# Attention scores in a macaron transformer block: the row minimum of tiles 2 and 3 taken with the sum over the relative scores, tile 0's scores in one product, a new order of the work

## The reference

```
x = x + 0.5 * ffn(layernorm(x))
x = x + attention(layernorm(x))
x = x + 0.5 * ffn(layernorm(x))

ffn(x) = sum over 8 experts of (silu(x @ Wg[e]) * (x @ Wu[e])) @ Wd[e]        # 128 -> 512 -> 128

attention, 16 heads of 8 features:
q, k = rotary(x @ w_q.T) / sqrt(8), rotary(x @ w_k.T);  v = x @ w_v.T
rel[i, j] = rel_emb[clip(j - i, -32, 32) + 32]
scores = q k^T + q . rel[i, j], causal;  p = softmax(scores)
ctx = p v + sum_j p[i, j] rel[i, j];  out = ctx @ w_o.T
```

## Time and profile before

| | us |
|---|---|
| median of 3 runs | 1436.86 (1435.93 to 1439.6) |
| the profiled execution, its own time | 1438.3 |
| its span | 1436.5 |
| TensorE busy | 1375.4 (96%) |
| VectorE busy | 1278.3 (89%) |
| ScalarE busy | 1101.9 (77%) |
| GpSimd busy | 1087.4 (76%) |

### The profile page before, as it was taken

One profiled execution on the slowest core, in us unless ns is written; L12 is line 12 of the kernel. 1 busy time (PEld: TensorE's weight loads), 2 busy tenths in 40 slices (PEclk: granted clock), 3 DMA queues, 4 the chain that ended last, 5 costly groups with the idle time before them and its releaser, 6 DMA issues.

```text
span 1436.5 us, 29572 instructions
## 1 busy us (share of the span) xinstructions
PE 1375.4 (96%) x8632; PEld 1076.9 (75%) x8632; DVE 1278.3 (89%) x2541; ACT 1101.9 (77%) x2642; POOL 1087.4 (76%) x956
## 2 busy tenths in 40 slices
PE   8999999999999999999999999999999999999898
PEld 7787676777777777777777778777777777778686
DVE  6887898999999999999999989899999999899565
ACT  6656778878778887788888878778887778788454
POOL 7967787787778877887778768787777877677555
PEclk9999999999999999999999999999999999999999
DMA  6404999999999999999999999899999999897200
GB/s 185 142 15 125 154 192 187 178 204 170 180 188 175 165 178 176 187 160 189 164 152 209 170 167 179 148 191 177 171 172 161 192 162 173 161 173 142 44 1 8
DMA packets 718386, 225.08 MB, mean 157 GB/s; under 512 B 652305, under 2 KB 697745, under 8 KB 718225
## 3 DMA queue, kind: packets, MB, share of 16 engines
q1 hardware_dynamic: 556224, 172.45, 72.9%
q10 hardware_dynamic: 162000, 50.75, 19.4%
HBM read 60.95 MB, written 69.86 MB: 91 GB/s over the span
## 4 chain that ended last, share of the span: by engine, by line
PE 47%; DVE 19%; ACT 9%; issue 7%; DMA 6%; ACTq 4%; SPq 4%; POOL 3%; POOLq 0%; DVEq 0%
PE work L708 9%; PE work L710 9%; PE work L709 9%; PE acc L786 5%; PE acc L787 4%; DVE hid L1071 4%; PE acc L791 4%; DMA probs_t<-probs 4%; DVE hid L1065 3%; DVE negmax L1167 3%; ACTq L1000 3%; PE work L839 3%; DVE work L1162 3%; ACT work L960 2%; DVE probs L1176 2%
## 5 line engine op out<-in xcount | busy, mean ns | idle before, releaser
L1218 POOL TENSOR_TENSOR hid_lo<-hid,hid_hi 128x512 fp32r<-128x512 f32 x512 | 663.5, 1302 | 215.6 <-ACT hid_hi L915 115.1
L909 ACT ACTIVATE hid<-work 128x512 f32<-128x512 f32 x512 | 310.1, 606 | 123.9 <-PE work L710 84.9
L1065 DVE SCALAR_TENSOR_TENSOR hid<-hid,work 128x512 f32<-128x512 f32 x512 | 345.7, 680 | 53.9 <-ACT hid L909 53.4
L1071 DVE TENSOR_TENSOR hid<-hid,work 128x512 f32<-128x512 f32 x512 | 346.6, 680 | 33.6 <-PE work L710 31.2
L915 ACT CAST hid_hi<-hid 128x512 fp32r<-128x512 f32 x512 | 320.1, 630 | 49.7 <-DVE hid L1071 30.8
L786 PE MATMUL acc<-hid_hi,wd 128*128 128x512 f32 x512 | 216.5, 423 | 12.4 <-ACT hid_hi L915 9.9
L1167 DVE TENSOR_REDUCE negmax<-work 128x1 f32<-128x384 f32 (+3 forms) x352 | 219.2, 634 | 1.2
L1233 POOL TENSOR_TENSOR probs<-exps,probs 128x512 f16<-128x512 f32 (+1 forms) x160 | 172.0, 1075 | 62.8 <-ACT probs L972 59.8
L708 PE MATMUL work<-xt,wg 128*128 128x512 f32 x512 | 207.0, 404 | 5.4 <-DVE xt L1040 1.5
L708 PE MATMUL work<-xt,wu 128*128 128x512 f32 x512 | 206.1, 402 | 2.8 <-DVE hid L1071 1.9
L791 PE MATMUL acc<-hid_lo,wd 128*128 128x512 f32 x512 | 204.1, 401 | 1.0 <-POOL hid_lo L1218 0.7
(11 more groups left out here) (97 smaller groups left out, 2184.5 us busy)
## 6 DMA issues: line engine op xcount, KB each, us to landing
prob_window_scratch<-probs SPq DMA_DIRECT2D x384, 80.0 KB, 3.5
rel_win<-rel_window_scratch ACTq DMA_DIRECT2D x250, 96.0 KB, 4.3
q_scratch<-rope SPq DMA_DIRECT2D x16, 512.0 KB, 4.2
qq<-q_scratch ACTq DMA_DIRECT2D x32, 256.0 KB
rel_window_scratch<-g_s SPq DMA_DIRECT2D x32, 256.0 KB, 5.1
k_scratch<-rope SPq DMA_DIRECT2D x16, 512.0 KB, 4.2
kk<-k_scratch ACTq DMA_DIRECT2D x32, 256.0 KB
prob_window_scratch<-probs SPq DMA_DIRECT2D x32, 256.0 KB, 3.2
```

The costliest lines, as they stand in the source:

```text
L909: act.activation(hid[:, arg % HB, :], work[bank_of["gate", arg]][:, :], ACT.Tanh, scale=0.5).then_inc(s_tanh, 1)
L1065: dve.scalar_tensor_tensor(out=hid[:, arg % HB, :], in0=hid[:, arg % HB, :], scalar=1.0, in1=work[bank_of["gate", arg]][:, :], op0=ALU.add ...
L1071: dve.tensor_tensor(hid[:, arg % HB, :], hid[:, arg % HB, :], work[bank_of["up", arg]][:, :], ALU.mult).then_inc(s_hid, 1)
L1218: pool.tensor_tensor(hid_lo[:, arg % 2, :], hid[:, arg % HB, :], hid_hi[:, arg % 2, :].bitcast(F32), ALU.subtract).then_inc(s_hlo, 1)
```

## The change

For tiles 2 and 3, `largest` now reduces only the keys that no window covers, 224 of 384 and 352 of 512 columns, into a new small tile `far`, and waits only for the scores. `near` then runs behind it as one `tensor_tensor_reduce`: it adds the window to the last 160 columns and takes the minimum of the results and of `far` at once, into `negmax`. The exponential of these tiles waits for `near`, and `shifted` follows `near`. Tiles 0 and 1 keep their order and forms.

Tile 0's scores are one product with the operands exchanged: the queries of the tile are stationary and the padded keys of all four heads (512 columns) move. So `q_pad` of tile 0 pads the keys and waits for their load. That of tile 1 waits for the queries' load.

The planner gets new durations for some steps, the dependencies of the above, no `after_short`, and a new table `LATER`.

```diff
-    LATER = {"acc": -30.5, "attention_sum": -109.4, "band_turn": -104.1, "band_values": 13.2, "down": -3.2,
...
+    LATER = {"acc": -126.3, "attention_sum": -93.6, "band_turn": 15.6, "band_values": 3.2, "down": -3.3,
...
-        step("ACT", 0.7, time, "ln_scaled", what, ("ln_shift", what))
+        step("ACT", 1.54, time, "ln_scaled", what, ("ln_shift", what))
...
-        step("PE", 0.9, end + 24, "project_v", t, ("ln_lo", ("ln2", t)))
+        step("PE", 1.3, end + 24, "project_v", t, ("ln_lo", ("ln2", t)))
...
-            step("ACT", 0.3, first - 28, "load_q", gg, ("qk_store", (t, 0)), ("qrel", back(gg, 2)),
+            step("ACT", 0.5, first - 28, "load_q", gg, ("qk_store", (t, 0)), ("qrel", back(gg, 2)),
...
-            step("ACT", 0.3, first - 14, "load_k", gg, ("qk_store", (t, 1)),
+            step("ACT", 0.5, first - 14, "load_k", gg, ("qk_store", (t, 1)),
...
-                step("ACT", 0.55, max(begin - 13, first - 13), "load_window", quad, ("qrel_store", gg),
+                step("ACT", 0.85, max(begin - 13, first - 13), "load_window", quad, ("qrel_store", gg),
...
-                step("POOL", 1.0, begin - 6, "q_pad", quad, ("load_q", gg),
+                step("POOL", 1.0, begin - 6, "q_pad", quad, ("load_q" if i else "load_k", gg),
...
-                step("ACT", 0.3, due[last_of(quad)] + 5, "load_band", quad, ("store_band", last_of(quad)),
+                step("ACT", 0.35, due[last_of(quad)] + 5, "load_band", quad, ("store_band", last_of(quad)),
...
-                 ("load_k", quad // NT), done_with(back(k, 2)))
-            step("DVE", 0.07 + HEADS[i] * (P if i == 0 else W) / (960 if i < 2 else 580), due[k] + 0.5, "near", k, ("scores", k),
-                 ("load_window", quad))
-            step("DVE", wide(columns), due[k] + 0.7, "largest", k, ("near", k))
-            step("ACT", HEADS[i] * 0.235 + columns / 1200, due[k] + 1, "exp", k, ("largest", k),
+                 ("load_q", quad // NT), ("load_k", quad // NT), done_with(back(k, 2)))
+            step("DVE", 0.07 + HEADS[i] * (P if i == 0 else W) / (960 if i < 2 else 500), due[k] + 0.5, "near", k, ("scores", k),
+                 ("load_window", quad), ("largest", k if i > 1 else None))
+            step("DVE", wide(columns if i < 2 else i * P - R), due[k] + 0.7, "largest", k, ("near" if i < 2 else "scores", k))
+            step("ACT", HEADS[i] * 0.235 + columns / 1200, due[k] + 1, "exp", k, ("largest" if i < 2 else "near", k),
...
-        if name in ("gate", "up", "down", "down_lo", "project") and (start > clock["PE"] or after_short):
+        if name in ("gate", "up", "down", "down_lo", "project") and start > clock["PE"]:
             takes += 0.1
-        if engine == "PE":
-            after_short = name == "scores" and TASKS[arg % NK][1] < 2
...
+        far = sb("negmax_far", [P, 4])
...
                     if places[0] == 0:
                         pe.wait_ge(s_qp, quad + 1)
-                    for n, a in enumerate(places):
-                        done = pe.matmul(bank[:, n * keys:(n + 1) * keys], q_pad[:, quad % 2, a, :],
-                                         kk[:, gg % 2, 0:keys], start=True, stop=True)
+                    if i == 0:
+                        pe.wait_ge(s_qld[gg % 2], 16 * (gg // 2 + 1))
+                        done = pe.matmul(bank[:, :], qq[:, gg % 2, 0:P], q_pad[:, quad % 2, :, :].rearrange(
+                            "p a k -> p (a k)"), start=True, stop=True)
+                    else:
+                        for n, a in enumerate(places):
+                            done = pe.matmul(bank[:, n * keys:(n + 1) * keys], q_pad[:, quad % 2, a, :],
+                                             kk[:, gg % 2, 0:keys], start=True, stop=True)
...
-                    act.wait_ge(s_max, arg + 1)
+                    act.wait_ge(s_max if i < 2 else s_near, arg + 1)
...
+                    else:
+                        dve.wait_ge(s_max, arg + 1)
+                        dve.tensor_tensor_reduce(out=near[:, :, 0], in0=near[:, :, 0], in1=window_of[:, :, 0],
+                                                 op0=ALU.add, op1=ALU.min, scale=1.0, scalar=far[:, arg % 4:arg % 4 + 1],
+                                                 accum_out=negmax[:, place:place + 1]).then_inc(s_near, 1)
...
+                    else:
+                        dve.wait_ge(s_sc, arg + 1)
+                        dve.tensor_reduce(far[:, arg % 4:arg % 4 + 1], heads[:, 0, 0:i * P - R], AX.X, ALU.min).then_inc(s_max, 1)
...
                     if i == 0:
+                        pool.wait_ge(s_kld[gg % 2], 16 * (gg // 2 + 1))
+                    if i == 1:
                         pool.wait_ge(s_qld[gg % 2], 16 * (gg // 2 + 1))
...
+                    source = (qq if i else kk)[:, gg % 2, i * P:(i + 1) * P]
```

## The result

The changed kernel took 1458.4 us (median of 5 runs, 1442.45 to 1462.67) against 1435.93 us before on the same chip: a ratio of 1.0139, with a 95% interval of 1.0108 to 1.0169. On a second occasion, beside other kernels, it was 1451.87 against 1435.74, 1.0122 (1.0081 to 1.0163). It is slower. I had forecast 1423 with a range that ended at 1446. The profiled execution took 1442.45 us (span 1440.6), so it is the kernel's fastest run, and its profile shows less of the loss than the median has.

The account below looks back on a forecast made before the run. VectorE, 93% busy in attention with TensorE beside it, was taken as near the limit. Half of VectorE's 21 us and TensorE's 7 us, 14 us, with due times at 0, gave 1423 us; range 1404 to 1446.

Parts of the forecast that it names:

- The parts: Shorter reductions remove 41.6 us from VectorE, the new sum adds 20.5; tile 0's single product removes 7 us from TensorE.
- The pair's net: VectorE's reduction and sum in tiles 2 and 3 together save 21 us, between 42 saved and 10 lost.
- How much of it reaches the end: Share of the engines' savings that shortens the run: half, giving 14 us off.
- the chain's 23%: Share of the two VectorE instructions' busy time on the chain that ended last, taken as the low end.
- my half: Half of VectorE's and TensorE's savings reaches the end, with VectorE 93% busy and TensorE beside it.
- The due times at nothing: The new table and durations rearrange all five lists; taken as 0, between 9 us gained and 18 us lost.
- the loose end from the stages: If all attention stages were as loose on VectorE as the first, attention would grow by 1.5%, 18 us.
- My sentence on the DMA queues: The new order adds or removes no traffic: the DMA queues carry the same 225 MB.
- The slower rival: GpSimd's tile-0 padding waits for a late keys' load, delaying its queue: 24 us lost, 1447 us; chance 0.14, including looser order.
- My signs of being wrong: Sum stepping over 0.5 us, q_pad waiting over 14 us for keys, or TensorE's ScalarE and GpSimd stalls absorbing VectorE's saving.
- The accumulator eats it: VectorE's new sum costs 0.2 us more, a net loss of 10 us there: 1438 us; chance 0.12.
- all of it counts: VectorE sets the pace and the order is as dense as the best stage: 34 us off, 1403 us; chance 0.08.

Follow-up runs that it names:

- experiment 5: Kernel before, lists untouched, with the two new VectorE instructions in place and the window's load issued behind the exponential: 1428.16 against 1435.74 us, 0.9954.
- experiment 6: Kernel before with tiles 2 and 3 reducing 160 columns fewer into an unread tile, their exponentials taking a constant: 1428.22 against 1435.74 us, 0.9943.
- experiment 10: Kernel before, its lists moved little, with both new VectorE instructions, window load behind the exponential, and tile 0 in one product: 1426.57 against 1434.2 us, 0.9935.
- experiment 3: Changed kernel's lists with the old sum, reduction, four tile-0 products and padded queries: 1449.27 against 1434.71 us, 1.0099.
- The mended queue: Changed kernel with each task's transpose issued behind its band store on SyncE's queue: 1440.15 against 1434.2 us, 1.0044.
- experiment 15: Changed kernel's lists with the old instructions, and each task's transpose behind its band store on SyncE's queue: 1448.67 against 1434.37 us, 1.0104.
- experiment 11: Kernel before with only TensorE's list reordered, the values' products up to 2 us earlier: 1448.41 against 1434.2 us, 1.0091.
- Experiment 4: Changed kernel planned anew with the table of due times of before: 1453.31 against 1434.71 us, 1.0117.
- experiment 8: Changed kernel run again unaltered, with its granted clock in each run: 1451.87 us (1443.43 to 1463.54).

## Why the prediction was wrong

*The parts* were sized well. The shorter reductions gave 165 and 169 ns for my 163. (Where I gave the old ones as 681 and 551 ns, the order is that of tile 3 and tile 2.) The sum with the minimum cost 0.07 us more for my 0.08, and 0.12 where the shifted copy follows: I had that copy lose the same 0.1 us as before, and it loses more. The trace of the changed kernel has a second record for each of the 256 new sums, the reading of an accumulator, of 0.14 us. The pair's net was 18 us for my 21.

*How much of it reaches the end* was a term that I got wrong. I took half of an engine's saving, with the chain's 23% as the low end. Experiments 5 and 6 measured 8 of 18 and 8 of 43 us, 42% and 18%, and by their intervals 18 to 55% and 10 to 28%. The chain's share is inside both and my half only inside the first. I passed over it because VectorE was 93% busy. A busy engine in a fixed order need not set the pace: its list waits for others at certain places, and time saved elsewhere can lengthen these waits. In experiment 6, with 43 us of work taken off VectorE, its waits over all its lines rose from 142 to 167 us. With 0.23 instead of 0.5 my sum would have been 6 us (0.23 x 28), where experiment 10 measured 8. (My own range has an error of this kind too: 24 us off is 1413, not 1409.)

*The due times at nothing* is the step that failed and turned the sign. "A change of order has no sign that the trace shows" was my reason. The new lists cost 15 us with the old instructions (experiment 3), inside the 18 us that I had put as the loose end from the stages but not in my sum. With the new instructions they cost 25 to 32 us (the changed kernel against experiment 10), which is outside it: they take back the 8 us and the rest is the loss. The sign could in part be read ahead: the diff flips the order of `p_turn` and `store_band` (due 13.8 + 2 against 13.2 + 2.5 before, 30.2 + 2 against 30.6 + 2.5 after), and I never compared the table's entries with each other. The planner has a sign as well: simulated with the old planner's durations, the old lists end at 1375.5 us and the new ones, with the old instructions in their places, at 1404.2. My sentence on the DMA queues spoke of their bytes, which did not change, and not of their order, which did.

*The slower rival* had the right side and the wrong place. GpSimd did not wait for the keys in the changed kernel at all: its waits have no line in which the load releases q_pad, and experiment 10 has one such wait. What stood in its place was a list that holds its engine for something late, as I had described, but for transposes and stores, on SyncE's queue, TensorE and ScalarE. The looser order that I had counted under this rival, with a chance of 0.14 in all, is what came. My signs of being wrong would not have caught it: TensorE's stalls for ScalarE and GpSimd fell from 34.5 to 24.8 us, and I had none for transfers. Only the sum's step of 0.5 us was passed, in the half of the tasks where the copy waits for it. *The accumulator eats it* fell with experiment 5, where the new sum has its second record and the kernel is faster, and *all of it counts* with experiment 6.

*What stays open.* The mended queue leaves 6 us over before, where the same instructions in the old order are 8 us under: some 14 us lie in the other new lists. They are the same 14 us with the old instructions (experiment 15). TensorE's wait for the transposes (12.4 against 4.3 us) is there, and experiment 11, which made such waits, lost 14 us. But its edit moved the products too, and no experiment took just these waits out of the new lists without another cost, so they are a likely cause and not a shown one. Experiment 4 leaves the new table out and keeps the new durations and dependencies, and it loses as much. So the table alone is not the cause, and which duration or dependency is was not tried.

## What to carry to other kernels

When a change brings a new schedule, price the schedule by itself. Put the new instructions in the old order and the old ones in the new order: here the parts gave 0.65% in the old order and the order cost 1.0% with the old instructions. The two do not add up: together they cost 1.2 to 1.4%, where the sum would be 0.3%. In a table of due times, compare the entries that compete for one queue: a difference that went from 0.1 us one way to 0.9 us the other swapped most of a queue's pairs. And for an engine in a fixed order, do not take the busy share as the worth of its time; the share of the last chain was nearer here (23%, beside a busy share of 93%, where 42% and 18% of the time saved were measured).

## What the runs showed that I had not expected

Place alone is a large cost. One load at the head of ScalarE's list, waiting for an instruction that had moved by one place, cost 77 us (1505.5 against 1428.2), over three times what the whole change lost.

Relieving an engine can bring nothing. In the unmended new lists the new instructions gained nothing (1451.87 with them and 1449.27 without), and with two neighbours of SyncE's queue swapped they gained 8.5 us.

A long wait of TensorE can be paid for again through the granted clock: 4.43 us of waiting was followed by 3.3 us at 0.51. After 3.01 us in experiment 8 it was 1.00. Over six runs of the changed kernel the clock's share of the loss was, by the estimate above, at most 8 us of 16.
